# A selective scan whose every second unit shares its input product between DVE, ACT and POOL, with four scan output buffers

## The reference, cut to what matters

```
def step(h, inp):
    dt, b_t, c_t, x_t = inp
    A_bar = jnp.exp(dt[:, :, None] * A)
    h = A_bar * h + (dt * x_t)[:, :, None] * b_t[:, None, :]
    y = jnp.einsum('ben,bn->be', h, c_t)
    return (h, y)
```

## Time and profile before

| what | value |
|---|---|
| median of 3 runs | 2145.34 us (2144.02, 2145.34, 2146.32) |
| span of the profiled execution, first to last instruction | 2143.9 us |
| busy over the span | PE 86%, DVE 77%, ACT 52%, POOL 47% |
| first product (L1872) to last (L1872), 63 units | 569.03 to 801.02 us |
| mean granted TensorE clock | 0.942 |

### The profile page before, as it was taken

One profiled execution on the slowest core, in us unless ns is written; L12 is line 12 of the kernel. 1 busy time (PEld: TensorE's weight loads), 2 busy tenths in 40 slices (PEclk: granted clock), 3 DMA queues, 4 the chain that ended last, 5 costly groups with the idle time before them and its releaser, 6 DMA issues.

```text
span 2143.9 us, 32414 instructions
## 1 busy us (share of the span) xinstructions
PE 1852.0 (86%) x12284; PEld 1195.9 (56%) x12284; DVE 1659.2 (77%) x2131; ACT 1124.7 (52%) x1868; POOL 1004.6 (47%) x386
## 2 busy tenths in 40 slices
PE   6989898876888986799999978898888777899998
PEld 4444454445444445576777745555555455677776
DVE  4666555539799997667778599999999999876666
ACT  2344544433534322255555557777677676655554
POOL 3367766732266751101000068888889889500000
PEclk9799999988899998799999998999999999999999
DMA  3111202000200001001000000000001000010000
GB/s 84 31 31 31 44 21 55 4 12 1 50 0 0 1 0 35 15 19 31 30 30 15 1 1 2 2 2 2 1 2 31 2 2 1 30 30 30 15 16 20
DMA packets 35680, 39.13 MB, mean 18 GB/s; under 512 B 5891, under 2 KB 22534, under 8 KB 35526
## 3 DMA queue, kind: packets, MB, share of 16 engines
q1 hardware_dynamic: 34998, 36.01, 6.7%
q10 hardware_dynamic: 528, 1.05, 0.2%
HBM read 21.05 MB, written 1.05 MB: 10 GB/s over the span
## 4 chain that ended last, share of the span: by engine, by line
PE 49%; issue 17%; DVE 17%; POOL 10%; ACT 4%; SPq 1%; DMA 1%; DVEq 0%; ACTq 0%; POOLq 0%; PEldq 0%
PE ps L46 9%; PE ps L48 8%; PE ps L47 8%; DVE negm L2641 6%; POOL AF L733 3%; PE ps L537 3%; PE ps L521 3%; PE ps L562 2%; PE ps L2553 2%; PE ps L2470 2%; POOL AF L1552 2%; POOL AR_plain L2446 1%; PE ps L2544 1%; POOL hc L1552 1%; PE ps L570 1%
## 5 line engine op out<-in xcount | busy, mean ns | idle before, releaser
L2641 DVE TENSOR_REDUCE negm<-ps 128x64 bf16<-128x1024 f32 x256 | 302.1, 1215 | 20.6 <-PE ps L2544 20.5
L733 POOL TENSOR_TENSOR AF<-AF 128x2048 f32<-128x2048 f32 (+3 forms) x73 | 234.2, 3208 | 154.6 <-ACT AF L673 148.5
L2446 POOL TENSOR_TENSOR AR_plain<-AF 128x2048 f32<-128x2048 f32 x64 | 261.8, 4095 | 31.7 <-ACT AF L2597 31.4
L46 PE MATMUL ps<-XH,AR 128*128 128x512 f32 x616 | 255.2, 414 | 13.7 <-DVE XL L251 4.0
L2605 ACT ACTIVATE AF<-ps 128x1024 f32<-128x1024 f32 x192 | 196.3, 1023 | 134.4 <-PE ps L2553 132.9
L47 PE MATMUL ps<-XL,AR 128*128 128x512 f32 x616 | 245.7, 399 | 0.0
L48 PE MATMUL ps<-XH,AR 128*128 128x512 f32 x616 | 245.5, 399 | 0.0
L673 ACT ACTIVATE AF<-ps 128x512 f32<-128x512 f32 (+1 forms) x304 | 155.5, 576 | 148.2 <-PE ps L524 86.9
L2553 PE MATMUL ps<-negm,ident_bf 128*128 128x512 bf16 x512 | 162.0, 400 | 80.0 <-DVE negm L2641 79.6
L2648 DVE TENSOR_REDUCE AF<-AF 128x128 f32<-128x2048 f32 x96 | 218.6, 2277 | 0.0
L285 POOL TENSOR_SCALAR var_eps<-mv 128x8 f32<-128x8 f32 x10 | 4.2, 421 | 369.6 <-DVE mv L262 369.5
(11 more groups left out here) (336 smaller groups left out, 4371.6 us busy)
## 6 DMA issues: line engine op xcount, KB each, us to landing
AR<-AR SPq DMA_DIRECT2D x96, 128.0 KB, 2.4
AF<-in_L_ffn_Wg_dram SPq DMA_DIRECT2D x21, 256.0 KB, 2.8
AF<-in_L_ffn_Wu_dram SPq DMA_DIRECT2D x21, 256.0 KB, 3.1
AF<-in_L_ffn_Wd_dram SPq DMA_DIRECT2D x21, 256.0 KB, 3.9
AF<-AF SPq DMA_DIRECT2D x16, 64.0 KB, 2.4
AF<-AR_plain SPq DMA_DIRECT2D x16, 64.0 KB, 2.4
AF<-in_L_attn_a_Wq_dram SPq DMA_DIRECT2D x1, 512.0 KB, 4.1
AF<-in_L_attn_a_Wout_dram SPq DMA_DIRECT2D x1, 512.0 KB, 9.2
```

The costliest lines, as they stand in the source:

```text
L46: pe.matmul(out, ah, bh, start=start, stop=False)
L733: pool.tensor_tensor(zacc[u % 2][:, :, c0:512], zacc[u % 2][:, :, c0:512], pt[t % 4][:, :, 0:w], ALU.add).then_inc(s0_zp, 1)
L2446: pool.tensor_tensor(p6[m % 3].rearrange("p (j q i) -> p j q i", j=HJ, i=2), e6[m % 4].rearrange("p (j q i) -> p j q i", j=HJ, i=2), w6i[: ...
L2641: dve.tensor_reduce(negm6[:, j % 4, :], bank(2 * (j % 3), 2).rearrange("p (j q i) -> p q j i", j=HJ, i=2), mybir.AxisListType.XY, ALU.max, ...
```

## The change

In every odd unit DVE's product covers the first bank alone (512 of 1024 steps). The second half goes another way: ACT copies bank 5 to SBUF (`take_drive`, called right after the odd unit's exponential), POOL multiplies the copy by B into the second half of `uu` (`input_half`), and DVE's scan of the odd unit waits for that as well (`s2_ug`). The copy has two buffers in `raws`. PE's drive of the following even unit also waits for the copy (`s2_pc`). On POOL, `input_half(u+1)` stands in front of the output product of the even unit u. The scan output has four buffers in turn, `hs[:, 0]`, `hs[:, 1]` and the two halves of `xp_a`, so that a scan waits for the output product of unit k-4 where it waited for that of k-2. Nothing else moves.

```diff
--- before.py
+++ after.py
@@ -1416,6 +1416,8 @@
         xc_a = tp(EC, L)
         sk_a = tp(EC, L)
         dtr_b = tp(L)
+        hss = [hs[:, 0, :], hs[:, 1, :], xp_a[:, 0, 0:L], xp_a[:, 1, 0:L]]
+        pxs = [raws[:, 0:512], raws[:, 512:1024]]
         hcs = [hc[:, 0, :], hc[:, 1, :], dA[:, 0, :], dA[:, 1, :]]
 
         def by_c(v):
@@ -1456,6 +1458,8 @@
         s2_px = sem("s2_px")
         s2_dA = sem("s2_dA")
         s2_u = sem("s2_u")
+        s2_pc = sem("s2_pc")
+        s2_ug = sem("s2_ug")
         s2_h = sem("s2_h")
         s2_hc = sem("s2_hc")
         s2_yg = sem("s2_yg")
@@ -1544,12 +1548,23 @@
                     wait(pool, s2_px, NG * (p - 1))
                     pool.tensor_tensor(dxl[:, c, :], dxp[p], f32(dxh[:, c, :]), ALU.subtract).then_inc(s2_lox, 1)
 
+            def input_half(k):
+
+                b, j = k // (EC * NG), k // 2
+                pool.wait_ge(s2_pc, j + 1)
+                if k % (EC * NG) == 1:
+                    pool.wait_ge(s2_bd, 16 * EG * (b + 1))
+                wait(pool, s2_h, k - 1)
+                pool.tensor_tensor(uu[:, 1, 512:L], pxs[j % 2], bbs[b][:, 512:L], ALU.mult).then_inc(s2_ug, 1)
+
             for u in range(NU):
+                if u % 2 == 0:
+                    input_half(u + 1)
                 pool.wait_ge(s2_h, u + 1)
                 if u % (EC * NG) == 0:
                     pool.wait_ge(s2_cd, 16 * EG * (u // (EC * NG) + 1))
                 wait(pool, s2_yg, u - 3)
-                pool.tensor_tensor(hcs[u % 4], hs[:, u % 2, :], ccs[u // (EC * NG)], ALU.mult).then_inc(s2_hc, 1)
+                pool.tensor_tensor(hcs[u % 4], hss[u % 4], ccs[u // (EC * NG)], ALU.mult).then_inc(s2_hc, 1)
                 if u // NG + 1 < NP:
                     ready(u // NG + 1, u % NG)
 
@@ -1645,6 +1660,8 @@
                 if n == 0:
                     pe.wait_ge(s2_lox, p + 1)
                 wait(pe, s2_u, k)
+                if k % 2 == 0:
+                    wait(pe, s2_pc, k // 2)
                 for i in range(2):
                     o = bank(4 + i)
                     pe.matmul(o, spread[:, g, :], dxh[:, c, 512 * i:512 * i + 512], start=True, stop=False)
@@ -1701,6 +1718,12 @@
             for lo, o in ((DT, 256), (DT + NS, 320)):
                 act.activation(wcat[:, :, lo:lo + NS], bank(1)[:, o:o + EC * NS].rearrange("p (c n) -> p c n", c=EC),
                                ACT.Copy).then_inc(s2_wc, 1)
+
+        def take_drive(act, k):
+            j = k // 2
+            act.wait_ge(s2_px, k + 1)
+            wait(act, s2_ug, j - 1)
+            act.activation(pxs[j % 2], bank(5), ACT.Copy).then_inc(s2_pc, 1)
 
         def s2_act(act, link, s):
             act.wait_ge(s2_sel, 4)
@@ -1789,6 +1812,8 @@
                 o = bank(2 * (k % 2), 2)
                 G = k // NG % EC * NG + ORDER[k % NG]
                 act.activation(o, o, ACT.Exp, scale=negA[:, G:G + 1]).then_inc(s2_dA, 1)
+                if k % 2:
+                    take_drive(act, k)
                 p, n = k // NG + 1, k % NG
                 if p < NP:
                     if p == EC and n == 0:
@@ -1869,11 +1894,15 @@
                 dve.wait_ge(s2_px, k + 1)
                 if k % (EC * NG) == 0:
                     dve.wait_ge(s2_bd, 16 * EG * (k // (EC * NG) + 1))
-                dve.tensor_tensor(uu[:, k % 2, :], bank(4, 2), bbs[k // (EC * NG)], ALU.mult).then_inc(s2_u, 1)
+                w = 512 if k % 2 else L
+                dve.tensor_tensor(uu[:, k % 2, 0:w], bank(4, w // 512),
+                                  bbs[k // (EC * NG)][:, 0:w], ALU.mult).then_inc(s2_u, 1)
                 dve.wait_ge(s2_u, k + 1)
                 dve.wait_ge(s2_dA, k + 1)
-                wait(dve, s2_hc, k - 1)
-                dve.tensor_tensor_scan(hs[:, k % 2, :], bank(2 * (k % 2), 2), uu[:, k % 2, :], 0.0,
+                if k % 2:
+                    dve.wait_ge(s2_ug, k // 2 + 1)
+                wait(dve, s2_hc, k - 3)
+                dve.tensor_tensor_scan(hss[k % 4], bank(2 * (k % 2), 2), uu[:, k % 2, :], 0.0,
                                        ALU.mult, ALU.add).then_inc(s2_h, 1)
                 if k % NG == 1 and k > NG:
                     gate(k // NG - 1)
```

## The result

The changed kernel takes **2153.01 us** (median of 6 runs, 2149.01 to 2155.91). The kernel before, run beside it on the same chip, takes 2145.74 (6 runs, 2144.02 to 2150.40). The ratio is **1.0030, with a 95% interval of 1.0016 to 1.0044**: slower by 7.3 us, more than the 0.2% that can be told. Forecast was no change, 2144.7 us in a range of 2140.5 to 2151.5. The range does not hold the result.

What follows compares the result with a forecast made beforehand. DVE's list was taken to bound the scan stage, PE nearly as long. Terms -6.4, +3.6, +2.9, -0.7, +0.4 and -0.4 summed to -0.6 us: span 2143.3, prediction 2144.7 us, range 2140.5 to 2151.5.

Steps and rivals of the forecast that it cites:

- 0.06 to DVE: End of POOL's half product to start of DVE's odd scan: a hand-over of 0.06 us.
- 6.48: Length in us taken for each of 16 undisturbed pairs, a gain of 0.40 each; the new chain itself gave 6.51.
- PE alone 6.45: Undisturbed pair: its length if only PE's chain set it, ending at T+6.34, plus 0.11, is 6.45 us.
- DVE alone 6.38: Undisturbed pair: its length if only DVE set it, with a one-bank product of 0.69, is 6.38 us.
- I take 2.00: POOL's output products from the new scan buffer at word 1032: 2.00 us each, between bounds of 2.00 and 2.37 (+2.5).
- POOL's lateness: Preparations behind units 3 and 5 delay the half product: pairs of 7.78, +0.90 over 6.88, four pairs, +3.6 us.
- The third preparation's pairs: Unit 8's preparation delays unit 9's output product and PE's collect: 8.1 where it took 7.14, three pairs, +2.9 us.
- The fourth's: Unit 11's preparation of 2.00 leaves POOL 0.2 late: pairs of 6.65, three of them, -0.7 us.
- Pairs with `gate`: Three pairs at phase changes: +0.2 in each of two, where ACT's copy comes later, and -0.4 in the third.
- A: Rival, 10%: POOL always has the half product ready, PE sets 6.45 per pair, 12.5 us off, 2132.8 us.
- B: Rival, 17%: half product of 1.26 (2149.6 us) or output products from word 1032 of 2.37; both, 2152 us.
- C: Rival, 13%: PE's clock falls in new idle gaps of 1.6 us; in 4 of 7 such pairs +6, 2151 us.

Runs made afterwards that it cites:

- e5_swap: As e4_select, but in shared units PE computes bank 5 of the drive first and ACT copies it before its exponential; ratio to the kernel before 0.9970.
- e2_offset: The changed kernel with the two new scan buffers moved to words 14 and 1038; ratio to the kernel before 1.0021.
- e10_again: The changed kernel measured and profiled once more, nothing altered; ratio to the kernel before 1.0029.
- e4_select: As e2_offset, but odd units 5, 7, 9, 11, 13 of the three preparing phases keep DVE's whole product; ratio to the kernel before 1.0010.
- e3_prep8: The changed kernel with the first two preparations of each phase cut from 1024 to 8 columns; ratio to the kernel before 1.0007.
- e1_buffers: The kernel before with only the four scan buffers, no shared product; ratio to the kernel before 1.0008.
- e7_swap_all: As e5_swap, but every odd unit shares its product; ratio to the kernel before 0.9988.

## Why the prediction was wrong, and where it was right

Forecast was -0.6 us on the stretch; the profile shows +5.4, so 6.0 us are to be found.

**The step that failed first: the hand-over from POOL to DVE.** The working took its "0.06 to DVE" from POOL to PE. It is 0.20. The trace of before could have warned of a part of it: in other stages it has four waits of DVE for POOL, with 0.10 to 0.11 us from the end of one to the start of the other (POOL L226 ends at 530.75, DVE L240 starts at 530.86); no row was taken from there. Everything ahead of it was right: drive over T+2.46, POOL at T+3.17, half product 1.09 for 1.08. So 13 undisturbed pairs take 6.59 to 6.69, 6.66 in the mean, and not 6.48: against 6.89 before, +2.3 on the forecast. Some 1.7 of it is the hand-over; another 0.4 is the step from 6.51, which the chain gave, to the 6.48 that was taken because PE might set some pairs. PE set none: all 32 odd scans waited for POOL, where "about 27" were counted. The last pair, which ends with the last scan, takes 6.76 where it took 6.96: +0.2. The working noted each 0.1 us of the half product as 2.7 us in all, but put that uncertainty on the product alone, and gave the hand-over none. The steps "PE alone 6.45" and "DVE alone 6.38" were right; e5_swap reaches both.

**The second: output products from word 1032.** The step "I take 2.00" was wrong; they take 2.39 as those from word 0 do. The rule for word 0 was right, and so was its cost of nothing. The bound was right too: e2_offset's rest is 2.6 us shorter. This includes units 20 and 36, the pairs of the first preparation in the second and third phase, which were counted as undisturbed because a preceding wait for PE covers POOL. They took 7.03 and 7.45 (+1.5 together against the forecast), and 6.69 once the products were 2.00: the cover was there, but too thin for 0.4 us more.

**POOL's lateness was right.** The mechanism was forecast with its place and nearly its size: 7.78 against 7.95 three times and 8.33 once, together +1.1, from the two prices above. The third preparation's pairs took 7.95 for 8.1 (-0.5). The fourth's took 7.31 for 6.65 (+1.9): with output products of 2.00 they take 6.92, so 1.2 of it is word 1032 again, and the rest is the hand-over and lateness carried over, which I did not separate. Pairs with `gate` were right together, to 0.1. Those behind them are 0.5 shorter in this profile, but they differ by more than that from one profile to another.

Added up, each as the change of a group's pairs from before against the change that was forecast: 2.3 + 0.2 + 1.5 + 1.1 - 0.5 + 1.9 - 0.5 = +6.0, which is what was missing.

**What was forecast for the profile.** Right were one-bank products of 0.69 (0.67) and the half product. The scans of the late pairs start 1.66 us late in the pair shown, and 1.28 in the next one with a preparation, for 1.3. DVE's idle time before scans is 25.3 for 13, the clearest miss. The stretch is 5.4 from 235.5 and not within 3.

**The rivals.** A did not happen. B had two conditions: the half product of 1.26 is refuted, the products of 2.37 from word 1032 came true, and B gave 17% with 2152 for both together. C was seen in e10_again, but not in the first profile of the change, which had +5.4 without it. So the loss does not need C; it may be a part of why the medians (+7.3 and, in e10_again, +6.5) lie above what the first profile shows. That was not settled, as the profile shows one execution only.

The Trainium skill (GPSIMD Engine Reference, "Performance versus the Vector engine") would have made the half product 1.12. Measured is 1.09. For 1024 elements its 4497 ns for 2048 halves to 2.25, and the runs show 2.00 or 2.39, by where the inputs begin. Neither decides: with 1.12 the forecast would have been +0.6, still no change.

**What the loss comes to.** The prediction's size of the gain was thin from the start: 0.40 in 16 pairs against preparations in 10. With the hand-over it was 0.22 a pair, as e4_select shows, and the preparations cost about what was said (e3_prep8). The change loses because it puts a wait for POOL, which has a strict order of its own, into the chain of the engine that bounds: e3_prep8 takes the first two preparations out of that order, e5_swap shares the product only where POOL is on time and starts its chain earlier, and in both the loss is gone.

## What to carry to other kernels

When a change makes the bounding engine wait for a helper, price each hand-over in its own direction, from a wait of the same two engines anywhere in the trace, and give it bounds, as for the operation itself: 0.14 us too little is some 1.7 of the 6.0 us missed here in undisturbed pairs, and about 0.6 more in the four pairs of the first two preparations. Look in the helper's queue for what stands ahead of the new operation, and share the work only in units where nothing long does; begin the helper's chain as early as its input can be made (here one bank of the drive first), so that it ends before the bounding engine asks. Both together, with the new buffers moved as in e2_offset, turned +0.3% into -0.3%.

## What the runs showed of the hardware

- Hand-over from POOL to DVE: 0.20 us in the scans of this stage, 0.13 to 0.14 in its first two pairs (where one wait fewer stands before the scan), 0.10 to 0.11 at four places of other stages. The other directions, in this stage, are PE to ACT 0.03, ACT and DVE to POOL 0.08, POOL to PE 0.06.
- A POOL product of two 128x1024 inputs in SBUF takes 2.39 to 2.40 us with the first input at word 0 or 1032, and 2.00 at words 14 and 1038, the second input unchanged (e1_buffers, e2_offset). Why, no run tells.
- Idle times of PE of 1.76 us can be followed by a granted clock of 0.60 (e10_again), those of 1.75 and 1.89 us by 1.00, in the same kernel. Even 3.10 us, followed by 0.61 before, was followed by 1.00 once (e7_swap_all, idle until 695.77, 696 to 700 us, collect 1.91). The Trainium skill (TensorE: Matmul & The Clock Gate, Part 1) ties the clock to how busy the array has lately been; the rows agree in that each fall inside a phase follows an idle stretch, but its length alone does not decide it.
